# Attention block on one core: VectorE copies the softmax seeds of odd steps, ScalarE those of even steps

## What is computed

```
xn = group_norm(x, 32 groups) * gn_w + gn_b
q, k, v = split(wqkv @ xn + bqkv)          # 8 heads of 64 channels
w = softmax(q^T k / 8)                     # 2304 x 2304 for each head
out = xn + wproj @ (w applied to v) + bproj
```

## Time and profile before

| | |
|---|---|
| median of three runs | 3850.76 us (3850.36 to 3852.95) |
| the profiled execution's own time | 3851.22 us |
| its span | 3849.5 us |
| TensorE matmuls busy | 3737.8 us, 97% |
| GpSimd busy | 2997.9 us, 78% |
| ScalarE busy | 2875.1 us, 75% |
| VectorE busy | 2222.4 us, 58% |
| mean granted TensorE clock | 0.994 of full speed |

### The profile page before, as it was taken

One profiled execution on the slowest core, in us unless ns is written; L12 is line 12 of the kernel. 1 busy time (PEld: TensorE's weight loads), 2 busy tenths in 40 slices (PEclk: granted clock), 3 DMA queues, 4 the chain that ended last, 5 costly groups with the idle time before them and its releaser, 6 DMA issues.

```text
span 3849.5 us, 74532 instructions
## 1 busy us (share of the span) xinstructions
PE 3737.8 (97%) x30004; PEld 2293.1 (60%) x30004; DVE 2222.4 (58%) x2820; ACT 2875.1 (75%) x4037; POOL 2997.9 (78%) x1639
## 2 busy tenths in 40 slices
PE   6999999999999999999999999999999999999998
PEld 3565565655856556555675656555567565656556
DVE  4555556556555555655645565565655655555553
ACT  2777777787577777778757777777876777777784
POOL 0788888788388888878838888887874888888894
PEclk9999999999999999999999999999999999999999
DMA  2000012021400001202140000120123000000014
GB/s 79 14 23 24 17 35 63 25 58 37 143 20 19 23 22 31 71 16 59 43 137 19 23 22 17 37 67 21 55 70 109 22 19 23 20 20 19 20 36 136
DMA packets 133673, 165.02 MB, mean 43 GB/s; under 512 B 61648, under 2 KB 110800, under 8 KB 132816
## 3 DMA queue, kind: packets, MB, share of 16 engines
q1 hardware_dynamic: 133328, 160.26, 13.4%
HBM read 122.17 MB, written 38.04 MB: 42 GB/s over the span
## 4 chain that ended last, share of the span: by engine, by line
PE 88%; DVE 3%; POOL 2%; issue 2%; ACT 2%; DMA 1%; SPq 1%; POOLq 0%; ACTq 0%; DVEq 0%
PE oacc L604 26%; PE scores L583 22%; PE pool_bank L531 14%; PE aux_banks L553 12%; PE pool_bank L543 7%; PE scores L684 4%; POOL denom L1140 2%; PE pool_bank L570 1%; DVE o_norm L1003 1%; DVE maxima L905 1%; ACT probs L789 1%; DMA out<-probs 1%; PE scores L531 1%; ACT scores L802 1%; PE scores L543 0%
## 5 line engine op out<-in xcount | busy, mean ns | idle before, releaser
L1140 POOL TENSOR_TENSOR denom<-denom,probs 128x768 f32<-128x768 f32 x1536 | 2822.4, 1838 | 463.9 <-ACT probs L789 275.0
L905 DVE TENSOR_REDUCE maxima<-aux_banks 128x2 f32<-128x512 f32 x1728 | 1655.9, 958 | 1413.8 <-PE aux_banks L553 1382.4
L789 ACT ACTIVATE probs<-scores 128x768 f32<-128x768 f32 x1728 | 1309.0, 810 | 683.7 <-PE scores L583 678.5
L802 ACT ACTIVATE scores<-seeds 128x768 f32<-128x768 f32 x1728 | 1340.3, 821 | 13.5 <-PE scores L591 10.0
L604 PE MATMUL oacc<-probs,vals 128*64 128x384 f32 x6912 | 1276.8, 489 | 0.0
L604 PEld LDWEIGHTS oacc<-probs,vals 128*64 128x64 f32 x6912 | 498.7, 137 | 499.8 <-issue 309.4
L553 PE MATMUL aux_banks<-k_hi,q_hi 64*128 64x512 f32 (+1 forms) x3456 | 691.5, 396 | 43.2 <-DVE maxima L905 35.6
L553 PEld LDWEIGHTS aux_banks<-k_hi,q_hi 64*128 64x128 f32 x3456 | 322.9, 183 | 629.0 <-issue 462.2
L583 PE MATMUL scores<-q_hi,k_hi 64*128 64x384 f32 x3456 | 597.0, 341 | 11.3 <-ACT scores L802 10.9
L583 PE MATMUL scores<-q_lo,k_hi 64*128 64x384 f32 x3456 | 587.5, 335 | 0.0
L583 PE MATMUL scores<-q_hi,k_lo 64*128 64x384 f32 x3456 | 587.4, 336 | 0.0
(11 more groups left out here) (91 smaller groups left out, 1559.1 us busy)
## 6 DMA issues: line engine op xcount, KB each, us to landing
seeds<-neg_rows SPq DMA_DIRECT2D x96, 384.0 KB, 3.5
xtile<-x SPq DMA_DIRECT2D x72, 384.0 KB, 3.2
att<-o_norm SPq DMA_DIRECT2D x96, 192.0 KB, 1.9
probs<-x SPq DMA_DIRECT2D x24, 768.0 KB, 4.8
out<-probs SPq DMA_DIRECT2D x24, 768.0 KB, 6.7
xtile<-att SPq DMA_DIRECT2D x12, 768.0 KB, 5.0
att_raw<-att SPq DMA_DIRECT2D x12, 768.0 KB, 6.5
neg_rows<-neg_cols SPq DMA_DIRECT2D x384, 0.8 KB
```

The costliest lines, as they stand in the source:

```text
L789: a(prob(s).rearrange("p (h n) -> p h n", n=N), scores[:, s % 2, :, 0:N], ACT.Exp, scale=SCALE).then_inc(probs_ready, 1)
L802: a(scores[:, s % 2, :, 0:N], seeds[blk % 2][:, :].rearrange("p (e n) -> p e n", n=N), ACT.Copy).then_inc(seeded, 1)
L905: v.tensor_reduce(maxima[:, :, qt, kc], aux_banks[:, :, 0:UNIT_KEYS[kc % 2]], AX.X, ALU.max)\
L1140: gp.tensor_tensor(acc, acc, prob(s), ALU.add).then_inc(added, 1)
```

## The change

Seeds of odd steps move from ScalarE to VectorE. VectorE gets a function `seed` of its own, a `tensor_copy` from `seeds` in SBUF to score slot 1 in PSUM. It stands at the end of the work of each odd step s, behind the unit's maximum and behind a piece of `take_recip` where the step has one, and serves step s + 2. Like the one removed, it waits for the exponential that frees the slot. Step 1 of each batch is seeded ahead of VectorE's stream. Odd seeds count on a semaphore of their own, `seeded_odd`; TensorE waits for the one or the other by the step's parity, and SyncE for both before it overwrites a buffer of seeds.

```diff
@@ send_max (SyncE)
                 if n >= 2:
-                    sp.wait_ge(seeded, PRIMED + KT * (n - 1))
+                    sp.wait_ge(seeded, PRIMED + KT // 2 * (n - 1))
+                    sp.wait_ge(seeded_odd, PRIMED + KT // 2 * (n - 1))
@@ make_scores (TensorE)
-                pe.wait_ge(seeded, PRIMED + BSTEPS * b + s + 1)
+                pe.wait_ge(seeded_odd if s % 2 else seeded, PRIMED + BSTEPS // 2 * b + s // 2 + 1)
@@ stream (ScalarE)
-                    for s in range(GS * i + 2, min(GS * i + 4, BSTEPS)):
-                        seed(s, b)
+                    if GS * i + 2 < BSTEPS:
+                        seed(GS * i + 2, b)
@@ projection (ScalarE)
                     if n == PJ - 3 and not last:
                         seed(0, b + 1, PRIMED + PJ * b + n + 1)
-                    if n == PJ - 1 and not last:
-                        seed(1, b + 1, PRIMED + PJ * b + n + 1)
@@ ahead of the batches (ScalarE)
-            for s in (o_saved, proj_saved, seeded):
+            for s in (o_saved, proj_saved, seeded, seeded_odd):
                 act.sem_inc(s, PRIMED)
...
-            for s in range(2):
-                seed(s, 0, PRIMED)
+            seed(0, 0, PRIMED)
@@ VectorE, new
+            def seed(s, b):
+
+                blk = s // KT
+                if s % KT == 1:
+                    dve.wait_ge(seeds_in[blk % 2], 16 * (BLOCKS // 2 * b + blk // 2 + 1))
+                if s == 1:
+                    dve.wait_ge(banks_opened, 1)
+                    dve.wait_ge(proj_saved, PRIMED + PJ * b)
+                else:
+                    dve.wait_ge(probs_ready, PROBS_PRIMED + BSTEPS * b + s - 1)
+                v.tensor_copy(scores[:, 1, :, 0:N], seeds[blk % 2][:, :].rearrange("p (e n) -> p e n", n=N))\
+                    .then_inc(seeded_odd, 1)
@@ stream (VectorE)
                         if s in STATS_STEPS and not last:
                             take_stats(STATS_STEPS[s], b + 1)
+                        if s % 2 and s + 2 < BSTEPS:
+                            seed(s + 2, b)
@@ batch (VectorE)
                 v.tensor_tensor(res_b, next_b, pb, ALU.add).then_inc(res_coefs_ready, 1)
+                seed(1, b)
                 stream(b, last)
```

More of the change, by code:

```diff
@@ L300, in attention_block_program @@
         seeded = sem("seeded")
+        seeded_odd = sem("seeded_odd")
         scores_full = sem("scores_full")
```

## The result

The changed kernel takes 3925.28 us, the median of four runs (3924.31 to 3926.15), against 3851.2 us (3850.36 to 3852.95), now from four runs too, for the kernel before: a ratio of 1.0192 with a 95% interval of 1.0178 to 1.0207. The forecast was 3924.5, 73.7 us above the median of three runs before; measured are 74.1 us.

The account below looks back on a forecast made before the run. TensorE, matmuls busy 97%, was taken as the bound, with VectorE's chain setting its pace in `o_norm` slots. 69.5 + 3 - 3 + 2.7 + 1.4 = 73.6 us on 3851.22 made 3924.8, given as 3924.5; range 3890 to 3960.

Parts of the forecast that it names:

- The place of the cost: Slots with `o_norm`, where VectorE's chain sets TensorE's pace: 79 slots at 0.88 us each, +69.5 us.
- The copy: One VectorE copy of 768 columns into PSUM: 0.97 us, bounds 0.57 and 1.23.
- Plain slots at nothing: Slots without `o_norm`: the copy fits, as TensorE has 0.78 us to spare; price zero.
- the last stretch hidden by GpSimd: The last five `o_norm`, where GpSimd adds without pause and is itself the bound: TensorE's stall is hidden.
- waits and semaphores at nothing: SyncE's wait for old seeds becomes two, TensorE's waits stay as many, no DMA is added: zero.
- Crowded slots: Slots with statistics and the like: some go over by 0.1 to 0.3 us, +3 us in all.
- starts of batches: Step 1's seed now stands behind VectorE's last addition: 0.9 x 3 = +2.7 us, and +1.4 at the first start.
- the relief: ScalarE loses 864 copies, so part of the 10.9 us of waits returns: -3 us, bounds 0 and -11.
- Blocking on GpSimd: Copies wait for GpSimd's additions, then shut GpSimd out, making it the bound: +190 us, near 4045; chance 6%.
- The faster case: `o_norm` finds the port free, below about 0.7 us, so scores don't wait, leaving ScalarE's relief: 3842; chance 5%.
- The clock: Each of 79 stalls brings TensorE's clock to its lower level, losing 0.94 us: +74 on top, 3999; chance 5%.

Follow-up runs that it names:

- f2: The changed kernel with ScalarE keeping the 92 odd seeds that stood behind o_norm, VectorE making the other 772: 3861.9 us, ratio 1.0026.
- h2: The changed kernel with o_norm's multiplication replaced by a transposition of recip into o_norm, leaving the product out: 3840.33 us, ratio 0.997.
- f3: The changed kernel with VectorE's copies cut to 4 of 768 columns, waits, order and count kept: 3841.71 us, ratio 0.9977.
- f4: The kernel before with ScalarE's odd seeds, except step 1 of a batch, cut to 4 of 768 columns: 3837.34 us, ratio 0.9963.
- e6: The changed kernel with the copy's target a spare tile in SBUF, so odd seeds don't reach PSUM: 4215.25 us, ratio 1.0945.

## Why the prediction was right

**The place of the cost: right, and shown.** 79 slots at 0.88 us were forecast, 69.5 us. It is 68 slots at 0.85 in the mean, 57.6 us, and 8.4 in the three at slot 140, which the forecast had at 0.88 each; the other 16 give 1.2 back. That makes 64.8. f2 removes it by moving 92 copies, h2 by removing the wait ahead of them.

**The copy** takes 0.95 us; the rows gave 0.97. The estimate of 0.86 from the Trainium skill was too short. Its row (VectorE: DVE Perf Modes, The TRN2 errata) is for a target in SBUF, and the section says itself that the row comes out short and that about 150 cycles were measured as the fixed part; I had left that out.

**Plain slots at nothing** (-0.2), **the last stretch hidden by GpSimd** (+0.5), **waits and semaphores at nothing** (4.4 us in f3, with the short copies' length): right to within these few us.

**Three small terms were mis-sized, and they cancel.** Crowded slots cost 8.1 us for 3, starts of batches 5.9 for 4.1 (first slot included), and the relief gave back 6.1 in the normalization slots for 3. With the 4.7 too much behind `o_norm` the sum is 73.0 for 73.6. In this sum each term with bounds lies within them; but the relief alone, 14 us in f4, exceeds the 11 I gave as its bound. That the sum is right within 1 us is luck: it is more than this working deserved, and 5 to 10 us would have been fair.

**The rivals.** Blocking on GpSimd did not happen, and e6 shows its price: 364 us, not 190, by another path. The faster case needed an `o_norm` without wait, and in the changed kernel its median stayed at 1.64 us. h2 shows that the condition was right, but that its 3840.3 us stands so near the 3842 given is luck: the 3842 was the relief alone, and h2 is 20 us shorter behind `o_norm` and 16 longer at statistics and starts of batches, terms that the case did not have. The clock stayed up behind the stalls of 0.85 us in the streams. It fell behind one of the three stalls at slot 140, and at two starts of batches, which is the next section but one.

## What to carry to other kernels

Work handed to a half-idle engine costs nothing where that engine has room and its whole length where it already paces the bound one, so count the latter slots and leave their share where it was. Ahead of an instruction that waits for another engine's to end there is room for something else, but the wait comes in whole instructions of the other engine, so look where the boundary falls. Hand over only what frees an engine where it is late: with 81 of the 864 copies the kernel is 12.6 us faster than before, with all of them 74.1 us slower.

## What the runs showed that I had not expected

**TensorE's clock behind stalls.** The changed kernel at the start of its third batch: timeline of TensorE, and two stretches of 2 us behind it (granted clock is the last number but two).

```profile
2024.97 0.39 PE L555 MATMUL aux_banks<-k_hi,q_hi 64*128 64x256 f32 x2 [1.18 <-ACT probs L852]
...
2026.90 0.69 PE L585 MATMUL scores<-q_hi,k_hi 64*128 64x384 f32 x2 [1.01 <-DVE scores L1021]
2027.39 0.52 PE L585 MATMUL scores<-q_hi,k_lo 64*128 64x384 f32 x2
...
2028.59 2.35 PE L533 MATMUL pool_bank<-xn,wq 128*64 128x384 f32 x8
```
```profile
2027.50:2029.50 2.00, 2.00 (x12) 1.05 (x10) 0.80 (x1) 1.23 (x2) 0.27 (x1) 0.50 0.62 224
2029.50:2031.50 2.00, 2.00 (x14) 0.89 (x14) 1.49 (x3) 0.29 (x1) 1.54 (x1) 0.79 0.00 0
```

The copy's stall of 1.01 us follows 1.18 us of idle time that was there before the change, and the clock stood at 0.50, its level of 1.2 GHz: scores at 0.52 us a pair for 0.34, eight projection matmuls in 2.35 us for 1.51. This slot is 2.4 us longer than before, more than twice the stall, and so is that of the fourth batch. At the start of the second batch the clock stayed at 1.00 behind idle times of 1.18 and 1.28 us, and the slot is 1.1 us longer. Two idle times of about 1 us close together can thus bring the clock down or not; 1.18 alone did not in the kernel before. One of about 2 us can do either too, as slot 140 shows in the first and the second batch:

```profile
685.46 0.69 PE L585 MATMUL scores<-q_hi,k_hi 64*128 64x384 f32 x2 [2.05 <-DVE scores L1021]
...
1649.04 0.45 PE L585 MATMUL scores<-q_hi,k_hi 64*128 64x384 f32 x2 [2.07 <-DVE scores L1021]
```

In the 2 us behind the first the clock stood at 0.50, and the slot is 3.8 us longer than before; behind the second it stood at 1.00, and the slot is 2.3 us longer. So where the clock fell it added 1.3 to 1.5 us to a stall. What decides was not tried.
